# A two-engine recurrence: PE's second and third block of products of each step change places

## The chip, the cores and the metric

The kernel runs on 1 core of one Trainium2 chip. The metric is the device time of one execution in microseconds (us), the median of several runs. Engines are named as the profile names them: PE is TensorE (its weight loads are listed apart as PEld), ACT is ScalarE, DVE is VectorE, POOL is GpSimd, SP is SyncE, whose queue (SPq) issues the transfers.

## The reference, cut to what matters

```python
# x: (32, 256, 256) = batch, steps, features; cond: (32, 256)
def layer0(v):                       # gate, then a wavelet transform there and back
    h = silu(cond @ W1.T + b1)
    gate = sigmoid(h @ W2.T + b2)[:, None, :]
    a = inverse_haar(haar(v) * gate) # every coefficient has the same gate
    return v + a
def layer1(x):                       # a plain recurrent layer over the steps, h0 = cond
    xW = x @ Wx + b
    for t in steps:
        h = tanh(h @ Wh + xW[:, t])
        out[:, t] = h
x = x + layer0(x)
x = x + layer1(x)
```

All gates of a feature are equal over the steps, so layer 0 is a factor: x becomes x * (2 + gate), one factor for each feature and batch row. The second layer is the work: 256 steps, each of which needs the h of the step before.

## The kernel before

Features lie on the partitions, in two halves of 128 (HALVES), and the 32 batch rows (B) on the free axis. A step t needs z = Wh^T h + Wx^T x_t + b for both halves m of the output features, and each of them sums over both halves k of the input features. So a step has four blocks of recurrent products, (k, m). Each is made by `recur` (L211 to L212), which calls `by_columns` (L183 to L187): four matmul instructions, each for 32 of the 128 output features, in float32, with a 128x32 moving operand. The trace counts eight weight loads and eight matmuls to a block, since a float32 matmul goes through PE in two passes. Since `by_columns` issues them all, every one of them has line L185.

Z lies in PSUM. `z_of(s, m)` gives the place of step s of a turn: half one (m = 0) in a bank called bank_e0 or bank_e1, for the steps 0 to 3 or 4 to 7 of a turn of 8 (TURN), half two (m = 1) in one of the four banks bank_l. The profile leaves the numbers out: bank_e is half one of z, bank_l half two. ACT reads z and writes tanh of it into h_ring (L172), half one first and then half two, each after a wait for z_whole[m]. Its increment, h_ready[s][m], releases PE. Both halves of h are in h_ring: half k of it is the moving operand of the blocks (k, 0) and (k, 1).

The input part is laid into z ahead of time. Before the recurrent products of each step, PE issues the fill of that step, `fill(s, turn)` (L252 to L279): `lay_bias` puts the bias there (matmuls of b_parts with ones, which start the sum) and `lay_input` adds Wx^T x of several steps at once. These products are for steps up to eight ahead and need no h. The fill differs by s: s = 0 has none, s = 3, 4, 5 and 7 have twelve matmul instructions each, s = 1, 2 and 6 have eight. Steps 1 and 5 wait for input_ready, which DVE gives.

All of PE's loop is written out for one turn of 8 steps and run 32 times (TURNS, L282). In a step, its products come in the order (k, m) = (one, one), (one, two), (two, one), (two, two), k being the half of h:

```python
for s in range(TURN):
    fill(s, turn)
    for k in range(HALVES):
        pe.wait_ge(h_ready[s][k], turn)
        for m in range(HALVES):
            done = recur((s + 1) % TURN, k, m, h_ring[:, k, s * B:(s + 1) * B])
            if k == HALVES - 1:
                done.then_inc(z_whole[m], 1)
```

DVE scales the coming x by the gate into x_ring and x1 (L303), and adds h to x1 for every two steps (L315), after h_ready of half two. SP loads x in chunks of 16 steps and stores the sums. PE, ACT, DVE and SP each run their own queue in order. Semaphores join them.

Of the kernel before, what the change touches and what calls it, by code (L numbers as in the profile page):

```python
# [14 lines left out]
def build(nc, x, w1_cond, w2, wx, wh, b_rows, out):  # L15
    CHUNKS, HALVES, N = x.shape[1:]
# [11 lines left out]
    with ExitStack() as ctx:  # L28
# [3 lines left out]
        def sem(name):  # L32
            return ctx.enter_context(nc.semaphore(name))
# [70 lines left out]
        z_whole = [sem(f"z_whole_{m}") for m in range(HALVES)]  # L104

        h_ready = [[sem(f"h_ready_{s}{m}") for m in range(HALVES)] for s in range(TURN)]
# [69 lines left out]
        def _(pe):  # L176
# [16 lines left out]
            def gate_product(layer, k, m, w_t, operand):  # L193
                return by_columns(z_ps[layer][m], w_t[:, k, m * P:(m + 1) * P], operand[:, k, :],
                                  start=(k == 0), stop=(k == HALVES - 1))
# [8 lines left out]
            def lay_input(s, steps, k, m):  # L204
                stride = 2 if m else 1
                moving = x_ring[:, k, :].rearrange("p (s b) -> p s b", b=B)[:, s:s + (steps - 1) * stride + 1:stride, :]
                return by_columns(z_of(s, m, steps).rearrange("p (s b) -> p s b", b=B), wx_sb[:, k, m * P:(m + 1) * P],
                                  moving)


            def recur(s, k, m, h, start=False):  # L211
                return by_columns(z_of(s, m), wh_sb[:, k, m * P:(m + 1) * P], h, start=start, stop=(k == HALVES - 1))  # L212
# [3 lines left out]
            for m in range(HALVES):  # L216
                for k in range(HALVES):
                    if m == 0:
                        pe.wait_ge(w1_loaded[k], DMA)
                    done = gate_product(0, k, m, w1_t, cond_t)  # L220
# [3 lines left out]
            for k in range(HALVES):  # L224
                pe.wait_ge(silu_ready, k + 1)
                for m in range(HALVES):
                    done = gate_product(1, k, m, w2_t, silu2)
# [13 lines left out]
            for m in range(HALVES):  # L241
                for k in range(HALVES):
                    if m == 0:
                        pe.wait_ge(first_input_ready, k + 1)
                    done = lay_input(0, 2 if m else 4, k, m)
# [6 lines left out]
            def fill(s, turn):  # L252
                if s == 1:
                    pe.wait_ge(input_ready[1], turn)
                    lay_bias(4, 4, 0)
                    lay_input(4, 4, 0, 0)
                if s == 2:
                    lay_input(4, 4, 1, 0)
                    lay_bias(4, 2, 1)
                if s == 3:  # L260
                    lay_input(4, 2, 0, 1)
                    lay_input(4, 2, 1, 1)
                    lay_bias(5, 2, 1)
                if s == 4:
                    lay_input(5, 2, 0, 1)
                    lay_input(5, 2, 1, 1)
                    lay_bias(0, 4, 0)
                if s == 5:
                    pe.wait_ge(input_ready[0], turn)
                    lay_input(0, 4, 0, 0)  # L270
                    lay_bias(0, 2, 1)
                    lay_input(0, 2, 0, 1)
                if s == 6:
                    lay_input(0, 4, 1, 0)
                    lay_input(0, 2, 1, 1)
                if s == 7:
                    lay_bias(1, 2, 1)
                    lay_input(1, 2, 0, 1)
                    lay_input(1, 2, 1, 1)  # L279


            with nc.Fori(1, TURNS + 1, engines=bass.OrderedEngineSet([pe.engine]), head_slot={pe.engine: 0}) as turn:  # L282
                for s in range(TURN):
                    fill(s, turn)
                    for k in range(HALVES):
                        pe.wait_ge(h_ready[s][k], turn)
                        for m in range(HALVES):
                            done = recur((s + 1) % TURN, k, m, h_ring[:, k, s * B:(s + 1) * B])
                            if k == HALVES - 1:
                                done.then_inc(z_whole[m], 1)  # L290

        @block.vector
        def _(dve):
# [115 lines left out]
```

## Time and profile before

| | us |
|---|---|
| median of 3 runs (199.9 to 201.95) | 200.63 |
| the profiled execution, its own time | 200.03 |
| its span, first to last instruction | 198.2 |
| PE busy, matmuls | 183.2 |
| PE busy, weight loads | 151.3 |
| DVE busy | 83.0 |
| ACT busy | 77.2 |

The time of an execution holds 1.8 us around the span. A busy time counts the union of an engine's records; matmuls overlap one another, and their ends are modelled, so PE's busy time is not work at its peak. The timeline merges neighbouring records of one kind: its second number is the time from the start of the first to the end of the last, and xN their count. In brackets stands how long the engine had idled and what ended it.

### The profile page before, as it was taken

How to read it: one execution, taken by the hardware profiler on the slowest of the kernel's cores; microseconds unless marked ns; L12 is line 12 of the kernel's file. 1: busy time of each engine (PE TensorE's matmuls, PEld its weight loads, DVE VectorE, ACT ScalarE, POOL GpSimd, SP SyncE). 2: the span in 40 equal slices, each digit the busy share in tenths (PEclk: the TensorE clock that was granted, in tenths of full speed). 3: DMA queues.
4: the chain of work that ended last, by engine and by line, in shares of the span. 5: the costliest groups of instructions: out<-in, count | busy, mean ns of one | idle time of the engine just before them, and what ended most of it. 6: DMA issues, size and time to landing. Idle time of an engine off the chain costs nothing.

```text
span 198.2 us, 25465 instructions
## 1 busy us (share of the span) xinstructions
PE 183.2 (92%) x12218; PEld 151.3 (76%) x12218; DVE 83.0 (42%) x267; ACT 77.2 (39%) x520; POOL 0.5 (0%) x5
## 2 busy tenths in 40 slices
PE   7776999999999999999999999999999999999996
PEld 4665888777778877777887777788777778887775
DVE  1632444444435344444434343444434343444441
ACT  4222333444444333444444433344444433334442
POOL 1000000000000000000000000000000000000000
DMA  5403999942002020201102020110202010020212
GB/s 161 168 7 88 318 408 416 379 197 106 0 26 80 0 107 0 106 0 45 61 0 106 2 107 0 61 45 0 106 0 106 0 77 31 0 106 0 107 53 53
DMA packets 6961, 17.99 MB, mean 91 GB/s; under 512 B 1443, under 2 KB 2726, under 8 KB 6950
## 3 DMA queue, kind: packets, MB, share of 16 engines
q1 hardware_dynamic: 6800, 17.71, 24.0%
q10 hardware_dynamic: 150, 0.15, 0.2%
q8 instruction: 4, 0.07, 0.1%
q14 instruction: 7, 0.06, 0.1%
HBM read 9.48 MB, written 8.39 MB: 90 GB/s over the span
## 4 chain that ended last, share of the span: by engine, by line
PE 90%; ACT 3%; issue 2%; DMA 2%; SPq 1%
PE bank_e L185 54%; PE bank_l L185 36%; ACT h_ring L172 3%; DMA wh_sb<-in_wh 2%; SPq L125 0%; SPq L124 0%; SPq L123 0%; SPq L122 0%
## 5 line engine op out<-in xcount | busy, mean ns | idle before, releaser
L185 PE MATMUL bank_e<-h_ring,wh_sb 128*32 128x32 f32 x4096 | 101.5, 201 | 8.1 <-ACT h_ring L172 8.1
L185 PEld LDWEIGHTS bank_e<-h_ring,wh_sb 128*32 128x32 f32 x4096 | 72.9, 110 | 37.6 <-ACT h_ring L172 24.4
L185 PE MATMUL bank_l<-h_ring,wh_sb 128*32 128x32 f32 x4096 | 96.2, 196 | 1.8 <-issue 1.8
L172 ACT ACTIVATE h_ring<-bank_e 128x32 f32<-128x32 f32 x256 | 50.6, 198 | 115.0 <-PE bank_e L185 115.0
L315 DVE TENSOR_TENSOR x<-x,h_ring 128x128 f32<-128x128 f32 x129 | 37.6, 291 | 106.0 <-ACT h_ring L172 106.0
L185 PEld LDWEIGHTS bank_l<-h_ring,wh_sb 128*32 128x32 f32 x4096 | 74.6, 113 | 1.9 <-issue 1.9
L185 PE MATMUL bank_l<-x_ring,wx_sb 128*32 128x64 f32 x2080 | 66.3, 224 | 0.7 <-issue 0.7
L185 PE MATMUL bank_e<-x_ring,wx_sb 128*32 128x128 f32 x1040 | 57.4, 282 | 0.0
L172 ACT ACTIVATE h_ring<-bank_l 128x32 f32<-128x32 f32 x256 | 50.2, 196 | 0.2 <-PE bank_l L185 0.2
L185 PEld LDWEIGHTS bank_l<-x_ring,wx_sb 128*32 128x32 f32 x2080 | 46.4, 111 | 0.9 <-issue 0.8
L185 PE MATMUL bank_l<-ones,b_parts 128*32 128x64 bf16 x520 | 31.6, 194 | 0.0
L303 DVE TENSOR_TENSOR x_ring<-x,g_t 128x256 f32<-128x256 f32 x63 | 26.3, 418 | 2.4 <-DMA x<-in_x 2.3
L303 DVE TENSOR_TENSOR x<-x,g_t 128x256 f32<-128x256 f32 x64 | 26.7, 418 | 0.0
L185 PEld LDWEIGHTS bank_e<-x_ring,wx_sb 128*32 128x32 f32 x1040 | 26.4, 110 | 0.0
L185 PEld LDWEIGHTS bank_l<-ones,b_parts 128*32 128x32 bf16 x520 | 19.7, 97 | 0.0
L185 PE MATMUL bank_e<-ones,b_parts 128*32 128x128 bf16 x260 | 17.1, 222 | 0.0
L185 PEld LDWEIGHTS bank_e<-ones,b_parts 128*32 128x32 bf16 x260 | 9.6, 97 | 0.0
L179 PE MATMUL bank_e<-ones 128*128 128x256 bf16 x10 | 2.3, 418 | 1.1 <-DVE ones L318 1.1
L179 PEld LDWEIGHTS bank_e<-ones 128*128 128x128 bf16 x10 | 1.3, 144 | 1.5 <-DVE ones L318 1.0
L154 ACT ACT_TABLE_LOAD x1 | 1.3, 1283 | 2.5 <-issue 2.5
L185 PE MATMUL bank_e<-ones 128*32 128x256 bf16 x20 | 1.5, 413 | 0.0
L185 PEld LDWEIGHTS bank_e<-w_t,wh_sb 128*32 128x32 f32 x16 | 0.3, 148 | 1.4 <-DMA wh_sb<-in_wh 1.4
(25 smaller groups left out, 9.7 us busy)
## 6 DMA issues: line engine op xcount, KB each, us to landing
x<-in_x SPq DMA_DIRECT2D x15, 512.0 KB, 9.7
out_dram<-x SPq DMA_DIRECT2D x15, 512.0 KB, 3.0
x<-in_x SPq DMA_DIRECT2D x1, 384.0 KB, 5.0
w_t<-in_w SPq DMA_DIRECT2D x1, 256.0 KB, 3.2
wx_sb<-in_wx SPq DMA_DIRECT2D x1, 256.0 KB, 4.5
wh_sb<-in_wh SPq DMA_DIRECT2D x1, 256.0 KB, 4.5
out_dram<-x SPq DMA_DIRECT2D x1, 256.0 KB, 2.1
w_t<-in_w_cond SPq DMA_DIRECT2D x1, 145.0 KB, 2.8
```

The source lines that it names most:

```text
L154: nc.scalar.activation(table_t[:], ones[:, 0:1], ACT.Tanh)
L172: nc.scalar.activation(h_ring[:, m, s * B:(s + 1) * B], z_of(s, m), ACT.Tanh)\
L179: nc.tensor.matmul(idle_ps, ones[:], ones[:, 0:1].to_broadcast([P, 256]), start=True, stop=True)
L185: done = nc.tensor.matmul(out[q:q + 32], weights[:, q:q + 32], moving, start=start, stop=stop, skip_group_check=True)
L303: return nc.vector.tensor_tensor(raw if in_place else ring, raw, g_t[:].unsqueeze(2).to_broadcast([P, HALVES, PART, B]), ALU.mult)
L315: nc.vector.tensor_tensor(x1[:, c, :, cols], x1[:, c, :, cols], h_ring[:, :, s * B:(s + steps) * B], ALU.add).then_inc(out_ready, 1)
```

## The change

Each step of PE's loop runs over the halves of z outside and the halves of h inside. The wait for half one of h stays ahead of the first block, and the wait for half two of h stands ahead of the second block, both in the pass for half one of z. The increment of z_whole[m] is on the second block of each half of z. The fill and everything on other engines are as they were.

```diff
--- before.py
+++ after.py
@@ -282,12 +282,13 @@
             with nc.Fori(1, TURNS + 1, engines=bass.OrderedEngineSet([pe.engine]), head_slot={pe.engine: 0}) as turn:
                 for s in range(TURN):
                     fill(s, turn)
-                    for k in range(HALVES):
-                        pe.wait_ge(h_ready[s][k], turn)
-                        for m in range(HALVES):
+
+                    for m in range(HALVES):
+                        for k in range(HALVES):
+                            if m == 0:
+                                pe.wait_ge(h_ready[s][k], turn)
                             done = recur((s + 1) % TURN, k, m, h_ring[:, k, s * B:(s + 1) * B])
-                            if k == HALVES - 1:
-                                done.then_inc(z_whole[m], 1)
+                        done.then_inc(z_whole[m], 1)
 
         @block.vector
         def _(dve):
```

PE's queue at steps 2 and 3 of a turn, before (half one of z of step 3 is in bank_e0, of step 4 in bank_e1; a row with x4 is a block's four instructions, and a block behind a wait is one row and a row x3; bank_l10 and bank_l11 are half two of later steps, bank_l01 of step 3):

```order
L185 MATMUL bank_e0<-h_ring,wh_sb 32x32 [waits h_ready_20]
L185 MATMUL bank_e0<-h_ring,wh_sb 32x32 x3
L185 MATMUL bank_l01<-h_ring,wh_sb 32x32 x4
L185 MATMUL bank_e0<-h_ring,wh_sb 32x32 [waits h_ready_21]
L185 MATMUL bank_e0<-h_ring,wh_sb 32x32 x3
L185 MATMUL bank_l01<-h_ring,wh_sb 32x32 x4
L185 MATMUL bank_l10<-x_ring,wx_sb 32x64 x8
L185 MATMUL bank_l11<-ones,b_parts 32x64 x4
L185 MATMUL bank_e1<-h_ring,wh_sb 32x32 [waits h_ready_30]
L185 MATMUL bank_e1<-h_ring,wh_sb 32x32 x3
L185 MATMUL bank_l10<-h_ring,wh_sb 32x32 x4
L185 MATMUL bank_e1<-h_ring,wh_sb 32x32 [waits h_ready_31]
```

The same place in PE's queue after the change:

```order
L185 MATMUL bank_e0<-h_ring,wh_sb 32x32 [waits h_ready_20]
L185 MATMUL bank_e0<-h_ring,wh_sb 32x32 x3
L185 MATMUL bank_e0<-h_ring,wh_sb 32x32 [waits h_ready_21]
L185 MATMUL bank_e0<-h_ring,wh_sb 32x32 x3
L185 MATMUL bank_l01<-h_ring,wh_sb 32x32 x8
L185 MATMUL bank_l10<-x_ring,wx_sb 32x64 x8
L185 MATMUL bank_l11<-ones,b_parts 32x64 x4
L185 MATMUL bank_e1<-h_ring,wh_sb 32x32 [waits h_ready_30]
L185 MATMUL bank_e1<-h_ring,wh_sb 32x32 x3
L185 MATMUL bank_e1<-h_ring,wh_sb 32x32 [waits h_ready_31]
L185 MATMUL bank_e1<-h_ring,wh_sb 32x32 x3
```

The block of bank_e behind h_ready_21 stands directly behind the one behind h_ready_20, and both blocks of bank_l follow it as one row of eight. The fill rows (x_ring, ones) keep their place behind them.

PE's queue at the end of the turn, step 7, before (bank_e0 and bank_l00 hold z of step 0 of the next turn):

```order
L185 MATMUL bank_l01<-ones,b_parts 32x64 x4
L185 MATMUL bank_l01<-x_ring,wx_sb 32x64 x8
L185 MATMUL bank_e0<-h_ring,wh_sb 32x32 [waits h_ready_70]
L185 MATMUL bank_e0<-h_ring,wh_sb 32x32 x3
L185 MATMUL bank_l00<-h_ring,wh_sb 32x32 x4
L185 MATMUL bank_e0<-h_ring,wh_sb 32x32 [waits h_ready_71]
L185 MATMUL bank_e0<-h_ring,wh_sb 32x32 x3
L185 MATMUL bank_l00<-h_ring,wh_sb 32x32 x4
L282 REGISTER_ALU
L282 COMPARE_AND_BRANCH
L28 UNCONDITIONAL_BRANCH
```

The end of PE's turn after the change:

```order
L185 MATMUL bank_l01<-ones,b_parts 32x64 x4
L185 MATMUL bank_l01<-x_ring,wx_sb 32x64 x8
L185 MATMUL bank_e0<-h_ring,wh_sb 32x32 [waits h_ready_70]
L185 MATMUL bank_e0<-h_ring,wh_sb 32x32 x3
L185 MATMUL bank_e0<-h_ring,wh_sb 32x32 [waits h_ready_71]
L185 MATMUL bank_e0<-h_ring,wh_sb 32x32 x3
L185 MATMUL bank_l00<-h_ring,wh_sb 32x32 x8
L282 REGISTER_ALU
L282 COMPARE_AND_BRANCH
L28 UNCONDITIONAL_BRANCH
```

Here too the first bank_l block moved behind the wait for half two of h, and nothing else did.

## Rows read from the trace of the kernel before

**Rows 1.** The page: busy time of PE, and the chain that ended last by engine
```profile
PE 183.2 (92%) x12218; PEld 151.3 (76%) x12218; DVE 83.0 (42%) x267; ACT 77.2 (39%) x520; POOL 0.5 (0%) x5
...
PE 90%; ACT 3%; issue 2%; DMA 2%; SPq 1%
```

**Rows 2.** The waits, whole span: engine, line, releaser; us in total, times, longest
```profile
ACT h_ring L172 <- PE bank_e L185: 115.0, 256, 2.9
...
PEld bank_e L185 <- ACT h_ring L172: 24.4, 95, 0.4
...
ACT h_ring L172 <- PE bank_l L185: 0.2, 1, 0.2
```

**Rows 3.** The timeline, one step: start us, us, engine, line, operation, names, shapes, count
```profile
100.32 0.16 PEld L185 LDWEIGHTS bank_e<-h_ring,wh_sb 128*32 128x32 f32 x8 [0.17 <-ACT h_ring L172]
100.32 0.27 PE L185 MATMUL bank_e<-h_ring,wh_sb 128*32 128x32 f32 x8
100.38 0.16 PEld L185 LDWEIGHTS bank_l<-h_ring,wh_sb 128*32 128x32 f32 x8
100.40 0.25 PE L185 MATMUL bank_l<-h_ring,wh_sb 128*32 128x32 f32 x8
100.44 0.17 PEld L185 LDWEIGHTS bank_e<-h_ring,wh_sb 128*32 128x32 f32 x8
100.47 0.25 PE L185 MATMUL bank_e<-h_ring,wh_sb 128*32 128x32 f32 x8
100.50 0.16 PEld L185 LDWEIGHTS bank_l<-h_ring,wh_sb 128*32 128x32 f32 x8
100.53 0.25 PE L185 MATMUL bank_l<-h_ring,wh_sb 128*32 128x32 f32 x8
100.56 0.30 PEld L185 LDWEIGHTS bank_l<-x_ring,wx_sb 128*32 128x32 f32 x15
...
100.79 0.20 ACT L172 ACTIVATE h_ring<-bank_e 128x32 f32<-128x32 f32 x1 [0.43 <-PE bank_e L185]
...
100.88 0.20 ACT L172 ACTIVATE h_ring<-bank_l 128x32 f32<-128x32 f32 x1
101.04 0.16 PEld L185 LDWEIGHTS bank_e<-h_ring,wh_sb 128*32 128x32 f32 x8
```

**Rows 4.** The timeline of ACT alone, first turn, then the last step
```profile
13.26 0.20 ACT L172 ACTIVATE h_ring<-bank_e 128x32 f32<-128x32 f32 x1 [1.14 <-PE bank_e L185]
...
16.74 0.20 ACT L172 ACTIVATE h_ring<-bank_e 128x32 f32<-128x32 f32 x1 [2.47 <-PE bank_e L185]
...
195.61 0.20 ACT L172 ACTIVATE h_ring<-bank_e 128x32 f32<-128x32 f32 x1 [0.43 <-PE bank_e L185]
```

**Rows 5.** The timeline of PE's weight loads, a step without fill and the next
```profile
103.91 0.16 PEld L185 LDWEIGHTS bank_e<-h_ring,wh_sb 128*32 128x32 f32 x8
...
104.63 0.16 PEld L185 LDWEIGHTS bank_e<-h_ring,wh_sb 128*32 128x32 f32 x8 [0.37 <-ACT h_ring L172]
```

**Rows 6.** The timeline of PE's weight loads, end of the longest fill, next step
```profile
102.86 0.28 PEld L185 LDWEIGHTS bank_l<-x_ring,wx_sb 128*32 128x32 f32 x8
...
103.19 0.16 PEld L185 LDWEIGHTS bank_e<-h_ring,wh_sb 128*32 128x32 f32 x8
```

**Rows 7.** The timeline: matmuls running at 9.50 and at 9.54, and ACT's first two
```profile
9.20 0.55 PE L185 MATMUL bank_l<-x_ring,wx_sb 128*32 128x64 f32 x12
...
9.31 0.55 PE L185 MATMUL bank_l<-x_ring,wx_sb 128*32 128x64 f32 x12
...
9.18 0.20 ACT L172 ACTIVATE h_ring<-bank_e 128x32 f32<-128x32 f32 x1 [2.92 <-PE bank_e L185]
9.60 0.20 ACT L172 ACTIVATE h_ring<-bank_l 128x32 f32<-128x32 f32 x1 [0.23 <-PE bank_l L185]
```

**Rows 8.** The timeline of ACT in the prologue
```profile
4.47 0.28 ACT L160 ACTIVATE z<-gate_bank,w_t 128x32 f32<-128x32 f32 x1
4.64 0.29 ACT L158 ACTIVATE tanh_z<-gate_bank,half_b 128x32 f32<-128x32 f32 x1
```

## The prediction

> **What bounds the kernel now.** I read the busy shares and the chain that ended last first [rows 1]. PE is busy 92% of the span and holds 90% of the chain, which looks like an engine that is the bound. It isn't: matmul records overlap and their ends are modelled. The list of waits [rows 2] shows the loop. ACT waits for bank_e (half one of z) in each of the 256 steps, 115.0 us in all, 0.45 us a step. Where PE has nothing else to do, its weight loads wait for the h that ACT makes (24.4 us, 95 times). No row of the list has PE waiting a second time within a step, and ACT waits for bank_l (half two) once only. So each step is a ring of two engines: PE products, ACT tanh, PE products.
>
> One step of the timeline [rows 3] gives the ring its lengths. PE starts on half one of h at 100.32. Weight loads of the four blocks (eight loads each) start at 100.32, 100.38, 100.44 and 100.50, and the fill's at 100.56: 0.06 us a block, also right after a pause. The third block, the second product into bank_e, completes half one of z: matmuls from 100.47, 0.25 long, so done at 100.72, which is 0.40 after the start. ACT starts at 100.79 (0.07 later), takes 0.20, ends at 100.99, and PE starts the next step at 101.04 (0.05 later). Sum: 0.15 + 0.25 + 0.07 + 0.20 + 0.05 = 0.72 us. Over the run: half one's tanh starts at 16.74 and at 195.61 us, 249 steps apart [rows 4], 178.87 / 249 = 0.7184 us a step. 256 of these are 183.9 of the span's 198.2 us. Most of the rest is the prologue and two pauses of PE in the first turn, in which ACT idles 1.14 and 2.47 us instead of 0.43 [rows 4], 2.75 us more than in two plain steps.
>
> Two things are not on the ring. The fill is not: the step at 103.91 has no fill behind it and PE idles, and the next one still starts 0.72 later [rows 5]. Half two of z is not: its last product starts 0.06 behind half one's (100.53 against 100.47), its tanh starts 0.09 behind (100.88 against 100.79), and the h that it makes would be needed only two blocks, 0.12, after the restart. So 0.03 us of slack lie there.
>
> **The change part by part.** It removes, adds and resizes nothing. Per step 16 matmul instructions, two waits, two increments and the fill stay. The second block (h half one into z half two) and the third (h half two into z half one) change places, so the wait for half two of h moves up by one block. The increment for half one of z moves up with the third block. ACT's, DVE's and SP's instructions are the same, and no DMA is moved.
>
> *Half one of z* now completes after two blocks, 0.06 us earlier. If this alone happened, the ring would be 0.66 us and the run 255 x 0.06 = 15 us shorter.
>
> *Half two of h* now gates the second block. Follow the time t at which PE starts on half two of h. Block two (into bank_e) loads from t, block three from t + 0.06, block four from t + 0.12. That is the same run of three blocks behind a restart as now, so block four's matmuls start at t + 0.15 and end at t + 0.40 [rows 3]. ACT's tanh of half two starts 0.07 later, takes 0.20 [rows 3], and PE wakes 0.05 later: t + 0.72. The ring through half one was "two more blocks, then ACT"; the ring through half two is now "two more blocks, then ACT". It was one block, plus the slack. The gain is given back in full by the half that had been off the path: 0.72 before, 0.72 after.
>
> Check that nothing else comes later than t + 0.72. Half one of z: block two's matmuls end at t + 0.27 (the first block after a restart lasts 0.27 in [rows 3]), ACT at t + 0.34, done t + 0.54, PE starts block one at t + 0.59, its loads are through at t + 0.65, and PE pauses 0.07 for half two. ACT's two starts are then 0.13 apart, more than the 0.09 it needs now. So PE stops twice a step where it stopped once, and the new stop is the one that counts.
>
> *The fill* has room from behind block four until block one must start. Before: loads from 0.24 after the restart to 0.72, room 0.48. After: from t + 0.18 to t + 0.66 (block one may start as late as that), 0.48. The longest fill's last group of loads is reported from 102.86 for 0.28, to 103.14, and PE restarts at 103.19 [rows 6]. It fits as it did; if it didn't, it would cost some 0.02 us in one step of eight, 0.6 us.
>
> *Ends.* At the first step both halves of h are there when PE comes to them, and the new ring begins 0.06 us later than the old; after the last step half two's tanh follows at once, 0.03 earlier than ACT lets it now. These are under 0.1 us together, and the pauses in the first turn stay.
>
> **Prices that the trace doesn't show.** (a) What half two's own path costs, product to tanh: in steady steps it is hidden behind ACT's spacing. From below it is the 0.07 of half one, from above 0.10 (100.78 to 100.88). Only the first step shows it alone [rows 7]: the bank_l matmuls begun at 9.20 to 9.22 are still running at 9.50 (a row that begins at 9.20) and gone at 9.54 (a row that begins at 9.31), so the sixteenth, which completes half two, ends near 9.53; the tanh starts at 9.60. That is 0.07, as for half one in [rows 3]. I take 0.07, and keep +0.03. (b) A wake-up right behind a block instead of behind the fill or a long pause: now a step that begins 0.05 behind the last load of a long fill (103.19) and one that begins after 0.37 of idle loads (104.63) both keep the 0.72 (103.19, 103.91, 104.63), so how long PE stood makes no difference [rows 5, 6]. From the matmuls' starts a restart costs 0.02 (0.08 to the second block, then 0.07, 0.06), and that is in the ring already; I keep -0.02 (pipe still warm) and +0.02 (it is paid twice), and take 0. (c) Two blocks in a row that accumulate into the same columns of bank_l: zero, since a block of four instructions is eight passes here [rows 3], two over the same columns close together at 0.06 / 8 = 8 ns. The nearest longer run is the fill's 15 loads in 0.19 us [rows 3], 13 ns each, but with 64 columns instead of 32; the whole difference would be 0.04 a step.
>
> Sum: 255 x (0.72 - 0.72) = 0. The profiled execution took 200.03 us (span 198.2 and 1.8 around it), so 200.0 by its own time; the three runs have a median of 200.63, 0.6 above. I forecast 200.6 on that scale. A measurement of this kernel can tell about 1%, 2 us, from no change; here that is only 8 ns a step.
>
> **Rivals.**
> *Half two is the slower half (slower).* Place: from the last product into bank_l to ACT. If the tanh's 0.09 gap now is not ACT's own spacing but half two's longer path, the new ring carries 0.03 more: 255 x 0.031 = 7.9 us, 208.5. It decides from 8 ns on. For it: the gap (0.09) is larger than the gap of the products (0.06). Against: the first step's 0.07 [rows 7]; and in the prologue ACT's back-to-back starts, for operands that had been complete, stand 0.17 apart at 0.28 and 0.29 each [rows 8], 0.11 less than their duration, as 0.09 is to 0.20. ACT's spacing explains the gap.
> The Trainium skill would put ACT's spacing lower: Perfetto Trace Analysis, in "Optimizing Scalar/DVE Operations", gives some 51 ns of overhead for ScalarE on PSUM, and ScalarE: Activation LUTs, in its rules for kernel authors, 0.83 ns an element, an estimate of 78 ns for 32 elements. By that ACT would have been free before 0.09 and this rival's 208.5 would hold; the trace, at the first step, speaks against it.
> *The second stop costs (slower).* PE's pause of 0.07 in mid-step makes a wake-up of its own. With (b)'s upper bound 255 x 0.02 = 5.1 us, 205.7; with half of it 203.2. For it: the changed ring is sensitive to a wake behind a block just issued, which no row shows. Against: restarts behind a long fill and behind 0.37 of idle look alike [rows 5, 6].
> *Warm restart (faster).* If PE's restart after 0.07 us of pause has no lag between loads and matmuls, the ring loses up to 0.02: 195.5. Against: loads run at 0.06 a block from the first on, and they set the pace.
> The Trainium skill's TensorE: Matmul & The Clock Gate, in "Step-by-step: what each phase is for", says that PE pulls weight loads ahead of matmuls in flight. If it pulled them past a waiting product, the pause would be used and this rival's 195.5 would come; but the trace has loads and matmuls waiting for ACT alike (100.32 for both), so I don't count on it.
> *It doesn't do what it says:* if half one's earlier z alone counted, 200.6 - 15 = 185. The data forbid it: every z needs both halves of the h before.
>
> **How the numbers follow.** Forecast (within 1%) 0.62. Half two slower 0.07; second stop costs over 1% 0.17; accumulation or fill 0.02: slower 0.26. Faster over 1%: 0.12, nearly all of it the warm restart. The time is that of no change, 200.6. The range goes down half way to the warm restart, 198.0, and up to the second stop's full price, 205.7, which leaves out the 208.5 and the lowest.
>
> **What would show it.** Right: tanh of half one 0.13 before that of half two; steps of 0.72; PE waiting for h twice a step, and ACT waiting for bank_l in every step; block one starts near 0.59 and block two near 0.72 after block two of the step before. Wrong: a step off by 0.01 or more. Then the segment that differs (product end to tanh, tanh to restart, restart to fourth block) names the rival.

## The result, and the profile after

The changed kernel takes 207.53 us (median of 6 runs, 207.1 to 208.14) against 200.25 us of the kernel before beside it: ratio 1.035, 95% interval 1.032 to 1.038. It is slower by 3.5%, 7.3 us. The forecast was no change, and 207.53 lies above the range's upper end, 205.7.

The page of the changed kernel: the span, then busy time, then the chain by engine.

```profile
span 205.3 us, 25465 instructions
...
PE 192.2 (94%) x12218; PEld 168.7 (82%) x12218; DVE 82.9 (40%) x267; ACT 94.3 (46%) x520; POOL 0.5 (0%) x5
...
PE 90%; ACT 3%; issue 2%; DMA 2%; SPq 1%
```

PE's busy share rose from 92% to 94% [rows 1], and the chain's shares stayed. Neither says where 7 us came from. The waits (engine, line, releaser; us in total, times, longest):

```profile
ACT h_ring L172 <- PE bank_e L185: 104.9, 256, 3.1
PEld bank_e L185 <- ACT h_ring L172: 14.6, 62, 0.3
PE bank_e L185 <- ACT h_ring L172: 6.0, 31, 0.2
...
ACT h_ring L172 <- PE bank_l L185: 0.2, 1, 0.2
```

Half one's tanh now waits 104.9 us for PE instead of 115.0 [rows 2], which looks like a gain. It waits less because the second tanh of the step before ends later. That second tanh seems to wait for bank_l no more than before. The last row is one wait, at the first step: a tanh's record is 0.20 long, the second one starts inside it, so after the first step ACT is never idle ahead of it and the list has no row for its lateness. My prediction asked for such a row and was wrong to.

One step of the timeline, the one without fill:

```profile
102.14 0.20 ACT L172 ACTIVATE h_ring<-bank_e 128x32 f32<-128x32 f32 x1 [0.39 <-PE bank_e L185]
102.30 0.20 ACT L172 ACTIVATE h_ring<-bank_l 128x32 f32<-128x32 f32 x1
102.39 0.32 PEld L185 LDWEIGHTS bank_e<-h_ring,wh_sb 128*32 128x32 f32 x16 [0.30 <-ACT h_ring L172]
102.39 0.43 PE L185 MATMUL bank_e<-h_ring,wh_sb 128*32 128x32 f32 x16 [0.19 <-ACT h_ring L172]
102.60 0.23 PEld L185 LDWEIGHTS bank_l<-h_ring,wh_sb 128*32 128x32 f32 x16
102.63 0.31 PE L185 MATMUL bank_l<-h_ring,wh_sb 128*32 128x32 f32 x16
102.73 0.12 PEld L185 LDWEIGHTS bank_e<-ones,b_parts 128*32 128x32 bf16 x4
...
102.88 0.20 ACT L172 ACTIVATE h_ring<-bank_e 128x32 f32<-128x32 f32 x1 [0.39 <-PE bank_e L185]
103.04 0.20 ACT L172 ACTIVATE h_ring<-bank_l 128x32 f32<-128x32 f32 x1
```

The tanhs of the step start at 102.88 and 103.04, 0.16 apart (0.09 in [rows 3]; I had 0.13). The record of PE's loads from 102.39 holds blocks one and two. Cut out, block two alone starts at 102.54 (PE's weight loads running between 102.56 and 102.59):

```profile
102.54 0.15 PEld L185 LDWEIGHTS bank_e<-h_ring,wh_sb 128*32 128x32 f32 x7
```

So PE begins half two of h at 102.54 (tanh of half two from 102.30, ended 102.49, and 0.05). Half one's tanh follows at 102.88, 0.34 behind, as predicted. Half two's two blocks: weight loads from 102.60, matmuls from 102.63 to 102.94, 0.40 behind, as predicted. Half two's tanh: 103.04, which is 0.10 behind the modelled end of its products and not 0.07. From 102.54 to 103.04 is 0.50, where I had 0.47. The rest of the ring is as before: 0.20 and 0.05.

ACT alone, half one's tanh in the seventh step and in the last:

```profile
17.27 0.20 ACT L172 ACTIVATE h_ring<-bank_e 128x32 f32<-128x32 f32 x1 [2.38 <-PE bank_e L185]
...
202.64 0.20 ACT L172 ACTIVATE h_ring<-bank_e 128x32 f32<-128x32 f32 x1 [0.39 <-PE bank_e L185]
```

(202.64 - 17.27) / 249 = 0.7444 us a step, against 0.7184 from [rows 4]. 0.026 x 255 = 6.6 us of the 7.1 that the span grew; 0.5 lies ahead of 17.27 (it was 16.74), where the pauses of the first turn are. These pauses differ from kernel to kernel, so below the length of a step carries the argument, and the total time only supports it. The granted clock was 1.00 in both profiled executions.

The tables below give medians over the steps between 60 and 190 us, in ns, from the starts of the same records before the timeline rounds them. Four numbers describe a step of the changed kernel: PE's start on half two of h to half one's tanh, 337; to half two's tanh, 496; tanh 198; tanh's end to PE's start, 51. In the kernel before: PE's start on half one of h to half one's tanh, three blocks later, 470; to half two's, 564.

### The profile page after: what moved, and what is told of

Read it like the earlier page. It is cut to its first block, busy times and chain, and to the rows that moved or that the text cites. A ratio compares the mean times of both kernels' runs of the same rounds, so it can differ in the third digit from the quotient of the medians.

```text
span 205.3 us, 25465 instructions
## 1 busy us (share of the span) xinstructions
PE 192.2 (94%) x12218; PEld 168.7 (82%) x12218; DVE 82.9 (40%) x267; ACT 94.3 (46%) x520; POOL 0.5 (0%) x5
## 4 chain that ended last, share of the span: by engine, by line
PE 90%; ACT 3%; issue 2%; DMA 2%; SPq 1%
PE bank_e L185 59%; PE bank_l L185 31%; ACT h_ring L172 3%; DMA wh_sb<-in_wh 2%; SPq L125 0%; SPq L124 0%; SPq L123 0%; SPq L122 0%
## 5 line engine op out<-in xcount | busy, mean ns | idle before, releaser
L185 PE MATMUL bank_e<-h_ring,wh_sb 128*32 128x32 f32 x4096 | 109.4, 207 | 7.8 <-ACT h_ring L172 6.0
L185 PEld LDWEIGHTS bank_e<-h_ring,wh_sb 128*32 128x32 f32 x4096 | 80.8, 108 | 29.0 <-ACT h_ring L172 14.6
L172 ACT ACTIVATE h_ring<-bank_e 128x32 f32<-128x32 f32 x256 | 50.7, 198 | 104.9 <-PE bank_e L185 104.9
L185 PE MATMUL bank_l<-h_ring,wh_sb 128*32 128x32 f32 x4096 | 80.0, 196 | 0.0
L185 PE MATMUL bank_l<-x_ring,wx_sb 128*32 128x64 f32 x2080 | 61.0, 222 | 0.7 <-issue 0.7
L185 PEld LDWEIGHTS bank_l<-h_ring,wh_sb 128*32 128x32 f32 x4096 | 58.5, 113 | 0.0
L185 PE MATMUL bank_e<-x_ring,wx_sb 128*32 128x128 f32 x1040 | 53.9, 279 | 0.0
L185 PEld LDWEIGHTS bank_l<-x_ring,wx_sb 128*32 128x32 f32 x2080 | 41.8, 112 | 0.8 <-issue 0.8
L185 PE MATMUL bank_l<-ones,b_parts 128*32 128x64 bf16 x520 | 27.7, 194 | 0.0
L304 DVE TENSOR_TENSOR x_ring<-x,g_t 128x256 f32<-128x256 f32 x63 | 26.3, 418 | 2.6 <-DMA x<-in_x 2.5
L185 PEld LDWEIGHTS bank_e<-x_ring,wx_sb 128*32 128x32 f32 x1040 | 23.2, 114 | 0.0
L185 PEld LDWEIGHTS bank_l<-ones,b_parts 128*32 128x32 bf16 x520 | 15.4, 99 | 0.0
```

The costliest lines, as they stand in the source:

```text
L172: nc.scalar.activation(h_ring[:, m, s * B:(s + 1) * B], z_of(s, m), ACT.Tanh)\
L185: done = nc.tensor.matmul(out[q:q + 32], weights[:, q:q + 32], moving, start=start, stop=stop, skip_group_check=True)
L304: return nc.vector.tensor_tensor(raw if in_place else ring, raw, g_t[:].unsqueeze(2).to_broadcast([P, HALVES, PART, B]), ALU.mult)
```

## The experiments

In each sketch the products of a step are in order: hA-zB means half A of h into half B of z. Before: h1-z1, h1-z2, h2-z1, h2-z2. Changed: h1-z1, h2-z1, h1-z2, h2-z2. `recur(z_at, k, m, h)` makes a block with k and m counted from 0: `recur(z_at, 1, 0, ...)` is h2-z1. `recur_part` and `recur_order` make some of its four quarters, those of a range and those of a list. The diffs are cut to the lines that matter, and "..." marks a jump. Theories are named by the letters that the expectations give them.

### What is slow about half two: its bank, its neighbours, or ACT

Run 1, every half exchanged, in PE, ACT and DVE:

```diff
-                    for m in range(HALVES):
-                        for k in range(HALVES):
-                            if m == 0:
+                    for m in (1, 0):
+                        for k in (1, 0):
+                            if m == 1:
...
-                for m in range(HALVES):
+                for m in (1, 0):
                     act.wait_ge(z_whole[m], t + 1)
```

> The changed order with the two halves exchanged everywhere: PE makes both blocks of half two of z first (bank_l), then both of half one (bank_e), ACT does half two first, PE waits for half two of h first, DVE waits for half one. In the changed kernel the second half's path from the modelled end of its products to its tanh is 0.10 us, and the step is 0.746 us. Theory A (the path is long because of bank_l, the place of that half of z): bank_l is now the first, bank_e the second, the second half's path is 0.07, the step 0.72, about 200 us. Theory B (it is long because the half's two blocks follow each other on PE with nothing between) and theory C (it is long because this tanh is ACT's second, started while the first runs): the path of bank_e is now 0.10, the step 0.746, 207 to 208 us.

Measured: 206.77 us, ratio 1.030 (1.023 to 1.038), step 744 ns. ACT of this run:

```profile
101.33 0.20 ACT L172 ACTIVATE h_ring<-bank_l 128x32 f32<-128x32 f32 x1 [0.39 <-PE bank_l L185]
101.49 0.20 ACT L172 ACTIVATE h_ring<-bank_e 128x32 f32<-128x32 f32 x1
```

Bank_l is now first and quick, bank_e is second, 0.16 behind, and slow: 496 ns, as the second half was. Theory A fell: the bank doesn't matter, the place in the step does. This run can't tell B from C.

Run 2, the order of before with its first two blocks exchanged: h1-z2, h1-z1, h2-z1, h2-z2.

```diff
-                        for m in range(HALVES):
+                        for m in ((1, 0) if k == 0 else (0, 1)):
```

> The order of before, but with the first two blocks exchanged: h half one into z half two, then into z half one, wait for half two of h, h half two into z half one, then into z half two. So the two blocks of half one of z follow each other, the first half is still on the ring with two more blocks ahead of its last, and half two's blocks are apart. Theory B (two blocks in a row into one half delay that half by 0.03): the tanh of half one starts 0.03 later after its products, the step is about 0.745, 207 us. Theories A (bank_l) and C (ACT's second tanh): nothing changes on the ring through half one, step 0.718, 200 us.

Measured: 200.67 us, ratio 0.999 (0.996 to 1.003), step 718 to 719 ns, 470 ns from PE's start to half one's tanh. Theory B fell: two blocks in a row into one half of z cost nothing. ACT of this run:

```profile
100.85 0.20 ACT L172 ACTIVATE h_ring<-bank_e 128x32 f32<-128x32 f32 x1 [0.43 <-PE bank_e L185]
100.95 0.20 ACT L172 ACTIVATE h_ring<-bank_l 128x32 f32<-128x32 f32 x1
```

Run 3, the order of before with an extra block ahead of h2-z2 (`extra()` is four matmul instructions of a weight by itself into an unused bank):

```diff
+                            if k == HALVES - 1 and m == HALVES - 1:
+                                extra()
                             done = recur((s + 1) % TURN, k, m, h_ring[:, k, s * B:(s + 1) * B])
```

> The order of before with one block more (four matmuls of a weight by itself into an unused bank) between the last block of half one and the last block of half two of z. Half two's last block then starts 0.12 instead of 0.06 behind half one's, so its tanh is held by its own products and not by ACT's spacing of 0.09. Half two's blocks are not in a row. Theory B (blocks in a row): half two's path is 0.07, its tanh starts 0.12 to 0.13 behind that of half one, the ring through half two is 2 blocks and 0.59, the step stays at 0.72, 200 to 201 us. Theories A and C: the path is 0.10, the tanh starts 0.155 behind, and the step grows to 0.745 to 0.75, 207 to 208 us.

Measured: 210.28 us, ratio 1.049 (1.041 to 1.057); the step is 744 ns (mean 745 between 60 and 190 us). The total is 3.5 us above run 1's, which has the same step; 2.7 of that lie in longer steps between 18 and 26 us, one of which took 2.49 us. ACT:

```profile
101.11 0.20 ACT L172 ACTIVATE h_ring<-bank_e 128x32 f32<-128x32 f32 x1 [0.39 <-PE bank_e L185]
101.27 0.20 ACT L172 ACTIVATE h_ring<-bank_l 128x32 f32<-128x32 f32 x1
```

The second tanh is 0.16 behind, as in the changed kernel, though half two's blocks aren't in a row. So the long path is already in the old order; there it was not on the ring.

Run 4, the changed order with two extra blocks between h2-z1 and h1-z2:

```diff
+                            if m == 1 and k == 0:
+                                extra()
+                                extra()
```

> The changed order with two blocks more (as above, into an unused bank) between the last block of half one and the first of half two, whose two blocks still follow each other. Half two's tanh then starts 0.28 behind that of half one, which takes 0.20, so ACT is idle by then. Theory C (ACT's second tanh starts late while the first runs): the path shortens to 0.07, the step is 0.746 + 0.125 - 0.03 = 0.84 us, about 232 us. Theories A and B: the path stays at 0.10, the step is 0.87, about 239.5 us.

Measured: 243.38 us, ratio 1.211 (1.202 to 1.221), step 878 ns. ACT:

```profile
100.54 0.20 ACT L172 ACTIVATE h_ring<-bank_e 128x32 f32<-128x32 f32 x1 [0.39 <-PE bank_e L185]
100.83 0.20 ACT L172 ACTIVATE h_ring<-bank_l 128x32 f32<-128x32 f32 x1
101.41 0.20 ACT L172 ACTIVATE h_ring<-bank_e 128x32 f32<-128x32 f32 x1 [0.39 <-PE bank_e L185]
```

The first tanh has ended 0.09 before the second starts, and the step (878) isn't theory C's 840; it is nearer the 870 of the others. An overlap on ACT isn't the cause. After these four runs A, B and C have fallen.

### How the distance grows

Runs 5 to 7 move one, two or three of the four matmul instructions of h1-z2 behind h2-z1. Run 5:

```diff
+                    recur(z_at, 0, 0, h[0])
+                    recur_part(z_at, 0, 1, h[0], 0, 3)
+                    pe.wait_ge(h_ready[s][1], turn)
+                    recur(z_at, 1, 0, h[1]).then_inc(z_whole[0], 1)
+                    recur_part(z_at, 0, 1, h[0], 3, 4)
+                    recur(z_at, 1, 1, h[1]).then_inc(z_whole[1], 1)
```

> From the order of before, one of the four matmul instructions of the second block (h half one into z half two) is moved behind the third block, so that half one of z is complete 0.016 us earlier and half two's products end 0.078 behind it instead of 0.063. In all runs so far the second tanh of a step starts either 0.094 behind the first (its products were ready by then) or at least 0.159 behind it, 0.159 too where its products would have allowed 0.13 to 0.15, while with 0.29 between them its own path is the short one. Theory D (ACT's second start has two slots, 0.094 where it is ready in time, and 0.159 where it comes later): gap 0.094, half two of h is in time, step 0.718 - 0.016 = 0.702, 196.5 us. Theory E (the second half's path costs a fixed 0.026 to 0.03 more, and before this was hidden behind ACT's spacing): gap 0.078 + 0.03 = 0.11, half two of h comes 0.11 behind, needed at 0.109: step 0.702 to 0.704, 196.5 to 197 us. Both alike here; it is the next two that tell them apart.

Run 6 has `0, 2` and `2, 4` in these two calls, run 7 `0, 1` and `1, 4`:

```diff
-                    recur_part(z_at, 0, 1, h[0], 0, 3)
+                    recur_part(z_at, 0, 1, h[0], 0, 2)
```

> Two of the four matmul instructions of the second block behind the third. Half two's products end 0.094 behind half one's. Theory D: if that still counts as in time the gap is 0.094 to 0.10 and the step 0.718 - 0.031 = 0.687, 192.6 us; if not, the gap is 0.159 and the step 0.744, 207 us. Theory E: gap 0.12, the step in between, 0.71, 199 us.

> Three of the four matmul instructions of the second block behind the third. Half two's products end 0.11 behind half one's. Theory D: gap 0.159, the step is that of the changed kernel, 0.744, 207 us. Theory E: gap 0.14, step 0.73, 203 us.

Measured: run 5, 199.38 us, ratio 0.993 (0.990 to 0.997), step 712 ns; run 6, 198.44 us, 0.990 (0.986 to 0.993), 712 ns; run 7, 203.09 us, 1.014 (1.010 to 1.017), 728 ns. Runs 6 and 7 came out as theory E had them. Run 5 missed both theories' step of 0.702 to 0.704; run 12 takes that up. ACT of run 5, whose second tanh is 0.11 behind, as theory E had it:

```profile
99.91 0.20 ACT L172 ACTIVATE h_ring<-bank_e 128x32 f32<-128x32 f32 x1 [0.40 <-PE bank_e L185]
100.02 0.20 ACT L172 ACTIVATE h_ring<-bank_l 128x32 f32<-128x32 f32 x1
```

Run 8, the changed order with one matmul instruction more between h2-z1 and h1-z2 (`extra(1)`, into quarter 0 of an unused bank):

```diff
                         done.then_inc(z_whole[m], 1)
+                        if m == 0:
+                            extra(1)
```

> The changed order with one matmul instruction more (into an unused bank) between the last block of half one and the first of half two. Half two's products end 0.016 later. Theory D: its tanh would have had to wait for the 0.159 anyway, so the gap stays 0.159 and the step 0.744, 207 us, the added work is free. Theory E (fixed addition): gap 0.175, step 0.760, 211 us.

Measured: 218.08 us, ratio 1.088 (1.085 to 1.091), step 779 ns, distance of the tanhs 193 ns.

Theory D fell with runs 5 to 8: with the changed kernel's, the distances are 109, 126, 143, 159 and 193, not two slots. Theory E (a fixed addition) is left, though run 8's step missed its 760 ns as well. The distances of the two tanhs, against the number of matmul instructions between the two last products:

```
instructions between     5     6     7     8 (changed, runs 1 and 3)    9 (run 8)   16 (run 4)
distance, ns           109   126   143   159                          193         292
27 + 16.6 x number     110   127   143   160                          176         293
```

So each matmul instruction takes 16.6 ns and the second tanh comes 27 ns more behind, wherever it stands. Run 8 alone is 17 above the line. Its extra instruction and the next one are both for quarter 0 of the columns, which may be one place lost; that was not tried apart and isn't shown.

### Whose 27 ns

Run 9, PE as before, ACT does half two first (DVE then waits for half one):

```diff
-                for m in range(HALVES):
+                for m in (1, 0):
                     act.wait_ge(z_whole[m], t + 1)
```

> PE in the order of before, but ACT makes half two's tanh first and half one's second (DVE then waits for half one). Measured so far, from PE's start on a half of h to the start of a tanh: 337 ns for the step's first tanh with 4 matmul instructions to its last product, 470 with 12, so 16.6 for each further instruction; for the step's second tanh 479, 496, 564 and 629 with 11, 12, 16 and 20, always 26 to 27 more than that line. Theory F (the 27 ns are ACT's: its second tanh of a step starts later, whatever it waits for): half two's tanh, now the first, starts 336 + 12 x 16.6 = 536 ns behind PE's start, the step is 536 + spacing of two ready tanhs (94 or less) + 248 = 878 or less. Theory G (the 27 ns are PE's: the last increment of a run of products comes later): it starts at 563, the step is 27 longer, up to 905 ns. The distance of the second tanh, whose products are long ready, is ACT's own spacing.

Measured: 246.43 us, ratio 1.225 (1.215 to 1.236), step 899 ns. PE's weight loads at its start on half one of h, then ACT:

```profile
102.04 0.16 PEld L185 LDWEIGHTS bank_e<-h_ring,wh_sb 128*32 128x32 f32 x8 [0.29 <-ACT h_ring L172]
...
102.60 0.20 ACT L172 ACTIVATE h_ring<-bank_l 128x32 f32<-128x32 f32 x1 [0.61 <-PE bank_l L185]
102.70 0.19 ACT L172 ACTIVATE h_ring<-bank_e 128x32 f32<-128x32 f32 x1
```

From 102.04 to 102.60: 563 ns by the medians, theory G's number, though it is ACT's first tanh of the step. The 27 ns are PE's. The second tanh, whose products are long ready, follows at 94 ns: that is ACT's own spacing.

Runs 10 and 11, the changed order with ACT waiting for both increments ahead of its first tanh, and then with one increment and one wait:

```diff
+                act.wait_ge(z_whole[0], t + 1)
+                act.wait_ge(z_whole[1], t + 1)
                 for m in range(HALVES):
-                    act.wait_ge(z_whole[m], t + 1)
```

> The changed order, with ACT's two waits both ahead of the first tanh, so that it starts only when half two's products are complete. From PE's start on half two of h to the first tanh, 12 instructions: theory F (ACT's second tanh) 469 ns, theory G (PE's last increment) 496 ns. The step is 248 + spacing (94 or less) + that: up to 811 against up to 838 ns.

```diff
+                act.wait_ge(z_whole[1], t + 1)
                 for m in range(HALVES):
-                    act.wait_ge(z_whole[m], t + 1)
...
-                        done.then_inc(z_whole[m], 1)
+                        if m == 1:
+                            done.then_inc(z_whole[m], 1)
```

> As the run before, but PE makes one increment a step, at the last product of half two, and ACT waits for it alone. Theory F: 469 ns to the first tanh, as the run before. Theory G: 496 if the last product's completion is late by itself, 469 if it is the second increment that makes it late.

Measured: 245.14 us, ratio 1.219 (1.209 to 1.229), step 892 ns; and 222.65 us, ratio 1.107 (1.098 to 1.116), step 807 ns. ACT of run 11 around PE's start on half one of h:

```profile
101.47 0.20 ACT L172 ACTIVATE h_ring<-bank_e 128x32 f32<-128x32 f32 x1 [0.52 <-PE bank_l L185]
101.56 0.19 ACT L172 ACTIVATE h_ring<-bank_l 128x32 f32<-128x32 f32 x1
...
101.72 0.14 PEld L185 LDWEIGHTS bank_e<-h_ring,wh_sb 128*32 128x32 f32 x5
...
102.28 0.20 ACT L172 ACTIVATE h_ring<-bank_e 128x32 f32<-128x32 f32 x1 [0.52 <-PE bank_l L185]
```

In run 11 half two of h is ready 88 ns behind half one (93 between the starts, and the second tanh is 5 shorter), so of the 558 ns from PE's start to the first tanh 470 count from half two of h. That is 12 instructions and no 27: with the first increment gone, the last product's is on time. Run 10 has 644 - 88 = 556 and fits neither theory (469 or 496). The trace says where the 60 ns more are: with two waits ahead of one tanh, one of them, that for half two's increment, is an instruction of ACT by itself (EVENT_SEMAPHORE, once in each of the 256 steps, 17 ns). It starts 494 ns behind PE's start on half two of h, near theory G's 496, and the tanh 62 ns behind it. So the run agrees with theory G as far as it goes. It doesn't prove it, since the record of a wait and that of a tanh may not start at the same point of a release.

Runs 13 to 15 add one increment of a semaphore that nobody waits for: at the end of h1-z1 in the order of before; at the end of h1-z2 in the changed order; at the end of h1-z1 in the changed order, ahead of PE's stop. Run 13:

```diff
+                            if k == 0 and m == 0:
+                                done.then_inc(spare, 1)
```

> The order of before, with one increment more: the last product of the step's first block increments a semaphore that nobody waits for. Theory H (each increment holds up the products behind it, or their completion, by 26 ns): from PE's start to half one's tanh 470 + 26 = 496 ns, step 718 + 26 = 744, 207 us. If an increment costs nothing: 470, 718, 200.5 us.

Run 14, in the changed order (run 15 has `m == 0`):

```diff
+                            if k == 0 and m == 1:
+                                done.then_inc(spare, 1)
```

> The changed order with the same spare increment, on the last product of the third block (h half one into z half two), between the increment of half one and that of half two. Theory H: from PE's start on half two of h to its tanh 496 + 26 = 522 ns, step 744 + 26 = 770, 213.5 us. If an increment costs nothing: 744, 207 us.

> The changed order with the spare increment on the step's first block, ahead of PE's stop for half two of h (its last product is issued 0.1 us before PE starts again). Theory H, with a stop absorbing the delay: step 744, 207 us. Theory H, with the delay kept over the stop: 770, 213.5 us. If an increment costs nothing: 744.

Measured: run 13, 207.56 us, ratio 1.037 (1.033 to 1.040), step 744 ns. Run 14, 213.52 us, 1.067 (1.061 to 1.074), step 770 ns. Run 15, 206.64 us, 1.031 (1.028 to 1.035), step 744 ns. Run 13, PE's weight loads at the start on half one of h and the tanhs that follow:

```profile
102.20 0.16 PEld L186 LDWEIGHTS bank_e<-h_ring,wh_sb 128*32 128x32 f32 x8
...
102.70 0.20 ACT L173 ACTIVATE h_ring<-bank_e 128x32 f32<-128x32 f32 x1 [0.46 <-PE bank_e L186]
102.79 0.20 ACT L173 ACTIVATE h_ring<-bank_l 128x32 f32<-128x32 f32 x1
```

102.20 to 102.70 is 496 ns, 26 more than before's 470, from one increment that no engine reads. Run 14, ACT, whose two tanhs are now 0.18 apart:

```profile
101.81 0.20 ACT L173 ACTIVATE h_ring<-bank_e 128x32 f32<-128x32 f32 x1 [0.39 <-PE bank_e L186]
101.99 0.20 ACT L173 ACTIVATE h_ring<-bank_l 128x32 f32<-128x32 f32 x1
102.58 0.20 ACT L173 ACTIVATE h_ring<-bank_e 128x32 f32<-128x32 f32 x1 [0.39 <-PE bank_e L186]
102.76 0.20 ACT L173 ACTIVATE h_ring<-bank_l 128x32 f32<-128x32 f32 x1
```

Here two increments stand ahead of half two's last product, and it is at 521 ns. In run 15 the extra one stands ahead of PE's stop, and half two's tanh is at 496, as without it. ACT of run 15, with tanhs 0.16 apart again:

```profile
101.82 0.20 ACT L173 ACTIVATE h_ring<-bank_e 128x32 f32<-128x32 f32 x1 [0.39 <-PE bank_e L186]
101.98 0.20 ACT L173 ACTIVATE h_ring<-bank_l 128x32 f32<-128x32 f32 x1
102.57 0.20 ACT L173 ACTIVATE h_ring<-bank_e 128x32 f32<-128x32 f32 x1 [0.39 <-PE bank_e L186]
```

Time alone doesn't wear the delay off. In run 15 the extra increment's product starts 0.16 us ahead of half one's last product and costs nothing. In run 4 half one's last product starts 0.30 us ahead of half two's, and its increment still costs 26 ns. What lies between in run 15 and not in run 4 is PE's stop.

### A version that is faster than both

Run 12, one late, with the quarters kept in turn:

```diff
+                    recur(z_at, 0, 0, h[0])
+                    recur_order(z_at, 0, 1, h[0], (0, 1, 2))
+                    pe.wait_ge(h_ready[s][1], turn)
+                    recur_order(z_at, 1, 0, h[1], (3, 0, 1, 2)).then_inc(z_whole[0], 1)
+                    recur_order(z_at, 0, 1, h[0], (3,))
+                    recur(z_at, 1, 1, h[1]).then_inc(z_whole[1], 1)
```

> The first split again, with the 32-column quarters kept in turn: block one 0,1,2,3; three of block two 0,1,2; block three 3,0,1,2; the late one 3; block four 0,1,2,3. In the first split quarter 0 followed after three others instead of four, and its half one's tanh started at 463 ns behind PE's start instead of 337 + 7 x 16.6 = 453. If each quarter takes an instruction only every fourth place, this order gives 453 and a step of 453 + 248 = 701 ns, 196 us, which beats before (718) and the changed kernel (744). If the quarters don't matter, it is the 712 ns and 199 us of the first split.

Measured: 196.82 us, ratio 0.977 (0.970 to 0.984), step 702 ns, so 2.3% below before, and the whole interval is below 1. ACT, and PE's start on half one of h between:

```profile
101.24 0.20 ACT L172 ACTIVATE h_ring<-bank_e 128x32 f32<-128x32 f32 x1 [0.40 <-PE bank_e L217]
101.35 0.20 ACT L172 ACTIVATE h_ring<-bank_l 128x32 f32<-128x32 f32 x1
101.94 0.20 ACT L172 ACTIVATE h_ring<-bank_e 128x32 f32<-128x32 f32 x1 [0.39 <-PE bank_e L217]
...
102.19 0.16 PEld L185 LDWEIGHTS bank_e<-h_ring,wh_sb 128*32 128x32 f32 x8
...
102.64 0.20 ACT L172 ACTIVATE h_ring<-bank_e 128x32 f32<-128x32 f32 x1 [0.40 <-PE bank_e L217]
```

One instruction less stands ahead of half one's last product, and half two of h comes (109 ns) when PE is through with the seven instructions ahead of it (about 110, by the starts of matmuls). In run 5 the same count took 463 ns instead of 453: the order of the quarters was worth 10 ns a step.

## Why the prediction was wrong

The time from PE's start on a half of h to a tanh is one line in all runs but three, with n the matmul instructions from that start to the product that completes the half, and i the increments that PE made between (the product's own not counted). The start is that on half two of h where PE stops for it, and else that on half one. The line's three constants are taken from before's half one and the changed kernel's two halves; the other rows test it:

```
337 + 16.6 x (n - 4) + 26 x i   ns           n    i   line   measured
before, half one                            12    0    470   470
before, half two (ACT's spacing holds too)  16    1    562   564
changed, half one                            4    0    337   337
changed, half two                           12    1    496   496
run 4, half two                             20    1    629   629
run 6, half two                             10    1    463   463
run 7, half two                             11    1    479   479
run 9, half two as ACT's first              16    1    562   563
run 11, half two, one increment             12    0    470   470
run 12, half one                            11    0    453   453
run 13, half one, spare increment           12    1    496   496
run 14, half two, spare increment           12    2    522   521
run 15, spare increment ahead of the stop   12    1    496   496
off the line:
run 5, half one (quarters out of turn)      11    0    453   463
run 8, half two (quarter 0 twice in a row)  13    1    512   530
run 10, two waits ahead of the tanh         12    1    496   556
```

Point by point, by the prediction's own steps:

- The ring of two engines, its 0.72 and that the fill isn't on it: right. The step without fill is as long as the others after the change too.
- "The gain is given back in full by the half that had been off the path": right in kind. PE stops twice a step, the first half's tanh is 0.34 behind PE's start on half two of h, and that start sets the step. Block counts and all other segments (0.40 to the end of the products, 0.20, 0.05) came out as written.
- Price (a), "what half two's own path costs", is the step that failed: I took 0.07 and kept 0.10 as the upper bound. It is 0.10: 26 ns more, 255 times, 6.6 us. The rival "half two is the slower half" had this, with 0.031 and 208.5 us; I gave it a chance of 7 in 100. The cause is none that I had written: not the bank, not ACT, but the increment that half one's last product makes ahead of half two's (runs 11 and 13 to 15).
- Why I set it aside. First, the first step's rows [rows 7]: 0.07 there rests on modelled ends of matmuls that are 0.31 long, a bad ruler for 0.03, and PE wasn't in its steady pace: four 64-column instruction records take 0.11 there (9.20 to 9.31), while later the fill's loads come at 13 ns each, by the prediction's own reading of [rows 3], so four in 0.05. Whether the slower pace hides an increment's 26 ns no run tests, so why that step shows no delay is open. Second, "ACT's spacing explains the gap". Run 9 shows that ACT's spacing is 94 ns indeed. But run 9 also shows half two's own path in the old order, 563 ns with ACT free, and that is 563 - 470 = 93 ns behind half one's: four instructions (66) and the increment (26) make 92. By chance the two limits coincide, and showing that one of them suffices didn't exclude the other.
- Two tanhs whose inputs are ready stand 94 ns apart in runs 9 and 10. The prediction's estimate of 78 ns from the Trainium skill's Perfetto Trace Analysis, "Optimizing Scalar/DVE Operations", and ScalarE: Activation LUTs, rules for kernel authors, is too low here by 16. The rival that hung on them has the measured time nearly right, but by another mechanism: ACT's spacing is the 94 ns that the prediction had, and half two is late all the same.
- One increment more costs 26 ns (run 13). The Trainium skill's TensorE: Matmul & The Clock Gate, section "The cost: per-tile semaphore tail", gives 26.3 ns for each increment, since increments are made one after another, and the trace agrees. The Trainium skill states it for the increments of one packed group; here an increment made 4 to 16 instructions earlier costs the same. This is the rule that spoke against the change, and the prediction didn't weigh it.
- Price (b), the second stop: 0, as taken. In run 11 PE needs 470 ns for twelve instructions behind its stop in mid-step, as before shows behind its longer pause. The rival "the second stop costs" fell, and "warm restart" with it: in the changed kernel's waits PE's weight loads wait for ACT as the matmuls do.
- Price (c), blocks in a row: 0, as taken. Run 2 has them in a row for half one (470, as before), and half two's 496 is the same in a row (changed) and apart (run 3).
- "Right: ... ACT waiting for bank_l in every step" was a bad test, since the list can't show a wait that lies under the record of the tanh before.

The range was too narrow at the top by its own bounds: price (a)'s upper end alone makes 208.5, and with 8 ns a step deciding between cases it should have been inside.

## What to carry to other kernels

Where two engines hand work back and forth in under a microsecond, count PE's increments on the path as well as its instructions: here each one made since PE's last stop put off the next signal by 26 ns, and that hid under the 94 ns spacing of the other engine. When a half that was off the path is moved onto it, measure that half's own path first (one run with a block of useless work ahead of it does it). Then balance: work that one half doesn't need goes behind it, until both halves arrive when the engine is ready for them (run 12).

## What the runs showed of the hardware

- An increment on a matmul puts off ACT's start on a later product by 26 ns, also where nobody waits for it (run 13), with 4 (run 9) to 16 (run 4) instructions between; two put it off by 51 (run 14). A stop of PE, 0.11 us from the last load's start to the next one's, makes that good (run 15). Whether the later product itself or only its signal is late, no run tells.
- A 32-column float32 matmul instruction with 32 moving columns takes 16.6 ns on the path (eight more of them from the changed kernel to run 4: 133 ns), while the reported starts of matmuls stand 0.06 / 4 = 15 to 16 ns apart. The four quarters of the columns in turn cost 10 ns less for eleven instructions than an order in which a quarter comes again after three (runs 5 and 12).
- Two tanhs of 128x32 from PSUM whose inputs are ready start 94 ns apart (runs 9 and 10), the first 198 ns long and the second 192.
- Of two waits ahead of one ACT instruction one became an instruction by itself, and the tanh started 62 ns behind its start (run 10; two runs and one trace, not followed up).
